# Three small tiles move in the order in which a fused attention and feed-forward kernel allocates its on-chip memory

## Chip, cores and metric

One core of one Trainium2 chip. The metric is the device time of the whole kernel in microseconds (us), the median of several runs. Engines are named as in the profile: PE is TensorE's matmul, PEld its weight load, DVE is VectorE, ACT is ScalarE, POOL is GpSimd, SP is SyncE, whose queue issues most of the DMAs.

## What is computed

The input x has 8 x 1024 tokens of 512 channels, the context 8 x 64 tokens of 384 channels. All weights are given.

```python
def reference(x, ctx, Wq, bq, Wk, bk, Wv, bv, Wo, bo, W1, b1, theta, w_real, w_imag, W2, b2):
    # layer 1: cross attention, 16 heads of 32 channels, 64 keys
    q = layernorm(x) @ Wq + bq;  k = ctx @ Wk + bk;  v = ctx @ Wv + bv
    attn = softmax(clip(q @ k.T * 32 ** -0.5, -1e4, 1e4))      # NaN anywhere: 1 / 64
    x = x + (attn @ v) @ Wo + bo
    # layer 2: feed-forward, 2048 hidden channels
    h = layernorm(x) @ W1 + b1
    g = cos(theta) * w_real + sin(theta) * w_imag
    act = relu(h + g * w_imag * sin(theta + 0.1 * h) * 0.1)
    return x + act @ W2 + b2
```

## The kernel before

All 8192 tokens are worked off in 16 tiles of 512 tokens, first all of them through the attention (phase A, 64 groups of 4 heads of a tile), then all of them through the feed-forward (phase B, 16 tiles by 16 chunks of 128 hidden channels). The order of the work on each engine is written out by hand, with a semaphore for each kind of hand-over.

Every large product is made of three matmuls. Each operand is split into a high part in the fp32r format and a low part that holds what is left, and `product` (lines 1040 to 1045) issues high by high, high by low and low by high into one bank of PSUM. The second operand of a matmul call is the moving one, which streams through the array; the first is the stationary one, which is loaded ahead of it.

- The normalised tile is transposed on PE (`transposes`, line 1049), copied out of PSUM by ACT as `xt_hi` (line 611), and DVE makes `xt_lo` of the rest (line 806).
- `queries` (line 1053) has `xt_hi` and `xt_lo` as moving operands against `wq_hi` and `wq_lo`: 12 matmuls of 128 x 512 for each of the 64 groups.
- Scores have `kbd` moving against `q` (128 x 256), the weighted values `pt` against `vbd`, the output projection `wo` against `o`.
- The first product of the feed-forward has `xt` moving again, against `w1a` or `w1b`: 12 matmuls for each of the 256 chunks. `second` (line 1234) has `w2` moving against `act`: 12 more.
- ACT reads the first product twice: `turns` with the bias `u_shift` (line 755) and `hid` with the bias `par` (line 757); DVE, POOL, ACT and DVE again make the sine and the activation of it.
- `minus_half` is the exponent tile of the reciprocal root on POOL (line 463). `par` holds the four vectors of 2048 channels, loaded at the start (line 603); `red` is scratch for them, `u_shift` and `gain` come of them (lines 942 to 955 and 998 to 1006).

Each tile on chip is a range of bytes that is the same in all 128 partitions. Tiles are laid one behind another in the order in which the program names them (lines 128 to 217), each at the next multiple of 32 bytes. The memory of phase A (`pa`) and that of phase B (`pb`) lie at the same place, 91168 and up. Start bytes as they come of the sizes, with the remainders that the text speaks of:

| tile | start | mod 64 | mod 512 |
|---|---|---|---|
| ident | 16512 | 0 | 128 |
| x_sb (2 tiles) | 23232, 31424 | 0 | 192 |
| par, u_shift, minus_half | 39616, 39872, 39936 | 0 | 192, 448, 0 |
| xt_hi, xt_lo | 39968, 48160 | 32 | 32 |
| bq_sb | 56672 | 32 | 352 |
| w1a, wq, kbd, act, w1b, w2, xn | from 58400 and from 91168 | 32 | 32 |
| wk_sb, wv_sb, ctxt | from 58400 | 32 | 32 |
| q, vbd, prob | behind kbd and two small tiles | 32 | 224 |
| pt, o, wo, res | behind three more small tiles | 32 | 96 |

Of the kernel before, what the change touches and what calls it, by code (L numbers as in the profile page):

```python
# [15 lines left out]
P = 128  # L16
# [12 lines left out]
NB = TOK // P  # L29
# [7 lines left out]
FC = FF // P  # L37
# [72 lines left out]
def xattn_ffn(nc, x, ctx_768, wq, bq, wk, bk, wv, bv, wo, bo, w1, b1, phases, w_real, w_imag, w2, b2,  # L110
# [5 lines left out]
    stack = ExitStack()  # L116
    with stack:
# [6 lines left out]
        def sbuf(where, name, shape, dt=F32):  # L124
            return where.enter_context(nc.sbuf_tensor(name, shape, dt))
# [5 lines left out]
        bo_row = sbuf(stack, "bo_row", [P, C])  # L131
        shift_rows = sbuf(stack, "shift_rows", [P, 2, NB])
        x_sb = [sbuf(stack, f"x_sb{i}", [P, NB, C]) for i in range(XBUFS)]
        par = sbuf(stack, "par", [P, 4, FC])
        u_shift = sbuf(stack, "u_shift", [P, FC])
        minus_half = sbuf(stack, "minus_half", [P, NB])
        xt_hi = sbuf(stack, "xt_hi", [P, KC, TOK], F32R)
        xt_lo = sbuf(stack, "xt_lo", [P, KC, TOK], F32R)
        stats = sbuf(stack, "stats", [P, 2, NB, 6])
        mv = sbuf(stack, "mv", [P, 2, NB, 2])  # L140
        var_eps = sbuf(stack, "var_eps", [P, 2, NB])
        rstd = sbuf(stack, "rstd", [P, 2, NB])
        bq_sb = sbuf(stack, "bq_sb", [P, KC])
        bk_sb = sbuf(stack, "bk_sb", [P, KC])
        red = sbuf(stack, "red", [P, 8, FC])
        gain = sbuf(stack, "gain", [P, FC])
        squares = sbuf(stack, "squares", [P, 2 * GROUPS])
        not_nan = sbuf(stack, "not_nan", [P, 2 * GROUPS])
# [1163 lines left out]
```

## Time and profile before

| | |
|---|---|
| median of 3 runs | 2117.81 us (2117.48 to 2121.49) |
| the profiled execution, its own time | 2117.81 us |
| its span, first to last instruction | 2116.1 us |
| outside the span | 1.7 us |
| TensorE, busy share of the span | 99% (2084.9 us) |
| mean granted clock of TensorE | 0.996 |

A matmul's record in this trace is longer than the time from its start to the start of the next, since matmuls are pipelined. So what a matmul costs is read from the distance of two starts in the timeline, not from its duration; the busy time of a group counts overlapping records of that group once, and sums over groups exceed the span.

### The profile page before, as it was taken

To read this page: it belongs to the slowest core of one execution; us is meant where nothing else is said; L and a number is where in the kernel's file an instruction comes from. 1 tells how busy PE (TensorE), PEld (TensorE's weight loads), DVE (VectorE), ACT (ScalarE), POOL (GpSimd) and SP (SyncE) were. 2 spreads that over 40 slices of the span, in tenths; PEclk is the share of its full clock that TensorE was granted. 3 is DMA by queue.
4 is the path that set the end of the run, shared out by engine and by line. 5 is a ranking of instruction groups with operands and counts; after the bars stand their busy time and mean duration, and the time that the engine had idled before them with its cause. 6 is when DMAs were issued, how large, how long until landed. Compare 5 with 4: busy or idle time off the path is not lost.

```text
span 2116.1 us, 27349 instructions
## 1 busy us (share of the span) xinstructions
PE 2084.9 (99%) x9986; PEld 1740.0 (82%) x9986; DVE 1313.4 (62%) x1994; ACT 1142.2 (54%) x2036; POOL 1040.0 (49%) x757
## 2 busy tenths in 40 slices
PE   7999999999999999999999999999999999999999
PEld 5888888888887878888888888888888888888887
DVE  5888888888875755555555555555545555555554
ACT  4766666766664655454454544445454444445543
POOL 4776777777775434353333533435334353443421
PEclk9999999999999999999999999999999999999999
DMA  5132232232213300101001010110101101011000
GB/s 180 56 105 80 86 105 95 76 105 75 75 56 120 100 31 20 40 1 41 14 27 40 1 40 1 40 41 1 41 1 41 40 1 40 1 40 40 1 20 21
DMA packets 54263, 102.49 MB, mean 48 GB/s; under 512 B 4840, under 2 KB 5352, under 8 KB 54128
## 3 DMA queue, kind: packets, MB, share of 16 engines
q1 hardware_dynamic: 52976, 100.17, 14.1%
q8 instruction: 79, 1.29, 0.3%
q10 hardware_dynamic: 1152, 0.56, 0.1%
q14 instruction: 56, 0.46, 0.1%
HBM read 66.10 MB, written 34.62 MB: 48 GB/s over the span
## 4 chain that ended last, share of the span: by engine, by line
PE 90%; ACT 3%; DVE 3%; issue 2%; DMA 1%; POOL 0%; SPq 0%; POOLq 0%; ACTq 0%; DVEq 0%
PE psum L1043 29%; PE psum L1045 28%; PE psum L1044 28%; PE psum L1124 2%; PE psum L1049 2%; DVE hid L989 1%; ACT turns L755 1%; ACT hid L757 1%; DMA ctx_sb<-in_ctx 0%; ACT act_hi L746 0%; DVE prob L896 0%; DVE top L902 0%; ACT frac L742 0%; ACT x_sb L623 0%; DVE total L882 0%
## 5 line engine op out<-in xcount | busy, mean ns | idle before, releaser
L584 POOL TENSOR_TENSOR frac<-turns,frac 128x512 f32<-128x512 f32 x256 | 332.2, 1298 | 859.6 <-DVE frac L1017 859.6
L989 DVE SCALAR_TENSOR_TENSOR hid<-frac,gain,hid 128x512 f32<-128x512 f32 x256 | 321.3, 1255 | 147.8 <-ACT frac L742 146.7
L1043 PE MATMUL psum<-w_hi,act_hi 128*128 128x512 f32 x1024 | 400.8, 391 | 0.0
L1044 PE MATMUL psum<-w_lo,act_hi 128*128 128x512 f32 x1024 | 399.4, 390 | 0.0
L1045 PE MATMUL psum<-w_hi,act_lo 128*128 128x512 f32 x1024 | 399.2, 390 | 0.0
L755 ACT ACTIVATE turns<-psum,u_shift 128x512 f32<-128x512 f32 x256 | 176.4, 689 | 372.0 <-PE psum L1045 330.3
L746 ACT ACTIVATE act_hi<-hid 128x512 fp32r<-128x512 f32 x256 | 161.8, 632 | 348.1 <-DVE hid L989 348.1
L1017 DVE TENSOR_SCALAR frac<-turns 128x512 f32<-128x512 f32 x256 | 109.8, 429 | 323.8 <-ACT turns L755 323.8
L992 DVE SCALAR_TENSOR_TENSOR act_lo<-hid,act_hi 128x512 fp32r<-128x512 f32 x256 | 196.4, 767 | 178.8 <-ACT act_hi L746 178.8
L1045 PEld LDWEIGHTS psum<-w_hi,act_lo 128*128 128x128 f32 x1024 | 192.9, 188 | 40.4
L1043 PEld LDWEIGHTS psum<-w_hi,act_hi 128*128 128x128 f32 x1024 | 192.9, 188 | 39.8
L1044 PEld LDWEIGHTS psum<-w_lo,act_hi 128*128 128x128 f32 x1024 | 192.9, 188 | 39.3
L1043 PE MATMUL psum<-xt_hi,w1a_hi 128*128 128x512 f32 x512 | 199.8, 390 | 0.0
L1044 PE MATMUL psum<-xt_lo,w1a_hi 128*128 128x512 f32 x512 | 199.6, 390 | 0.0
L1045 PE MATMUL psum<-xt_hi,w1a_lo 128*128 128x512 f32 x512 | 199.6, 390 | 0.0
L1045 PE MATMUL psum<-xt_hi,w1b_lo 128*128 128x512 f32 x512 | 199.3, 389 | 0.0
L1043 PE MATMUL psum<-xt_hi,w1b_hi 128*128 128x512 f32 x512 | 199.2, 389 | 0.0
L1044 PE MATMUL psum<-xt_lo,w1b_hi 128*128 128x512 f32 x512 | 199.2, 389 | 0.0
L528 POOL TENSOR_TENSOR prob<-prob,inv 128x1024 f32<-128x1024 f32 x64 | 122.0, 1906 | 112.9 <-DVE inv L884 112.9
L757 ACT ACTIVATE hid<-psum,par 128x512 f32<-128x512 f32 x256 | 174.5, 682 | 0.0
L742 ACT ACTIVATE frac<-frac 128x512 f32<-128x512 f32 x256 | 162.2, 633 | 0.0
L681 ACT ACTIVATE psum<-psum 128x512 f32<-128x512 f32 x128 | 74.5, 582 | 124.1 <-DVE prob L896 124.1
(143 smaller groups left out, 4190.9 us busy)
## 6 DMA issues: line engine op xcount, KB each, us to landing
res<-in_x SPq DMA_DIRECT2D x64, 256.0 KB, 2.8
x_dram<-res SPq DMA_DIRECT2D x64, 256.0 KB, 2.0
x_sb<-x_dram SPq DMA_DIRECT2D x16, 1024.0 KB, 5.5
x_sb<-in_x SPq DMA_DIRECT2D x15, 1024.0 KB, 5.7
out<-x_sb SPq DMA_DIRECT2D x15, 1024.0 KB, 4.2
stage<-in_w SPq DMA_DIRECT2D x32, 256.0 KB, 2.8
v_in<-v_dram SPq DMA_DIRECT2D x16, 128.0 KB, 3.0
x_sb<-in_x SPq DMA_DIRECT2D x4, 256.0 KB, 4.6
```

The costliest lines, as they stand in the source:

```text
L528: pool.tensor_tensor(rows, rows, inv[:, (i - 1) % 2, :].unsqueeze(2) .to_broadcast([P, NB * HG, KEYS]), ALU.mult).then_inc(prob_done, 1)
L584: pool.tensor_tensor(frac[:, j % 2, :], turns[:, j % 2, :], frac[:, j % 2, :], ALU.subtract)\
L742: act.activation(frac[:, j % 2, :], frac[:, j % 2, :], ACT.Sin, scale=SIN_SCALE).then_inc(sin_done, 1)
L746: act.activation(act_hi[:, j % ACTS, :], hid[:, j % 2, :], ACT.Relu).then_inc(act_hi_done, 1)
L755: act.activation(turns[:, j % 2, :], hidden, ACT.Identity, bias=u_shift[:, f:f + 1], scale=0.1 / TWO_PI).then_inc(turns_done, 1)
L757: act.activation(hid[:, j % 2, :], hidden, ACT.Identity, bias=par[:, 3, f:f + 1])\
L989: dve.scalar_tensor_tensor(out=hid[:, j % 2, :], in0=frac[:, j % 2, :], scalar=gain[:, f:f + 1], in1=hid[:, j % 2, :], op0=ALU.mult, op1=A ...
L992: dve.scalar_tensor_tensor(out=act_lo[:, j % ACTS, :], in0=hid[:, j % 2, :], scalar=0.0, in1=act_hi[:, j % ACTS, :].bitcast(F32), op0=ALU. ...
L1017: dve.tensor_scalar(frac[:, j % 2, :], turns[:, j % 2, :], ROUND, ROUND, ALU.add, ALU.subtract)\
L1043: pe.matmul(o, a_hi, b_hi, start=first, stop=False)
L1044: pe.matmul(o, a_hi, b_lo, start=False, stop=False)
L1045: return pe.matmul(o, a_lo, b_hi, start=False, stop=last)
```

## The change

Only the order of declarations changes. `par` and `u_shift`, which stood ahead of `xt_hi`, now stand around `red`, and `minus_half` stands behind `rstd`. No instruction, semaphore, shape or loop is changed.

```diff
         x_sb = [sbuf(stack, f"x_sb{i}", [P, NB, C]) for i in range(XBUFS)]
-        par = sbuf(stack, "par", [P, 4, FC])
-        u_shift = sbuf(stack, "u_shift", [P, FC])
-        minus_half = sbuf(stack, "minus_half", [P, NB])
         xt_hi = sbuf(stack, "xt_hi", [P, KC, TOK], F32R)
         xt_lo = sbuf(stack, "xt_lo", [P, KC, TOK], F32R)
         stats = sbuf(stack, "stats", [P, 2, NB, 6])
         mv = sbuf(stack, "mv", [P, 2, NB, 2])
         var_eps = sbuf(stack, "var_eps", [P, 2, NB])
         rstd = sbuf(stack, "rstd", [P, 2, NB])
+        minus_half = sbuf(stack, "minus_half", [P, NB])
         bq_sb = sbuf(stack, "bq_sb", [P, KC])
         bk_sb = sbuf(stack, "bk_sb", [P, KC])
+        par = sbuf(stack, "par", [P, 4, FC])
         red = sbuf(stack, "red", [P, 8, FC])
+        u_shift = sbuf(stack, "u_shift", [P, FC])
         gain = sbuf(stack, "gain", [P, FC])
```

What it does to the start bytes, by the same rule:

| tile | start before | start after | mod 64 after | mod 512 after |
|---|---|---|---|---|
| xt_hi | 39968 | 39616 | 0 | 192 |
| xt_lo | 48160 | 47808 | 0 | 192 |
| stats, mv, var_eps, rstd | 56352 to 56671 | 56000 to 56319 | 0, 0, 0, 32 | |
| minus_half | 39936 | 56320 | 0 | |
| bq_sb, bk_sb | 56672, 56704 | 56352, 56384 | 32, 0 | |
| par | 39616 | 56416 | 32 | |
| red | 56736 | 56672 | 32 | |
| u_shift | 39872 | 57184 | 32 | |
| gain and all that follow, and all that stand ahead of par | as before | as before | | |

## Rows read from the trace of the kernel before

**Rows 1.** The page: busy time by engine, then granted clock in 40 slices.

```profile
PE 2084.9 (99%) x9986; PEld 1740.0 (82%) x9986; DVE 1313.4 (62%) x1994; ACT 1142.2 (54%) x2036; POOL 1040.0 (49%) x757
...
PEclk9999999999999999999999999999999999999999
```

**Rows 2.** The page: shares of the chain that ended last, by engine.

```profile
PE 90%; ACT 3%; DVE 3%; issue 2%; DMA 1%; POOL 0%; SPq 0%; POOLq 0%; ACTq 0%; DVEq 0%
```

**Rows 3.** Stretches of phase A (first) and B: length, busy time, clock, DMA.

```profile
100.00:500.00 400.00, 397.53 (x2209) 342.72 (x2208) 343.60 (x574) 269.62 (x537) 295.71 (x212) 1.00 0.27 89
...
1500.00:2000.00 500.00, 499.77 (x2242) 414.12 (x2241) 264.50 (x374) 244.72 (x405) 200.96 (x141) 1.00 0.08 26
```

**Rows 4.** Groups: line, engine, operation, tiles, shape, count; busy us, mean ns; idle before.

```profile
L1043 PE MATMUL psum<-xt_hi,w1a_hi 128*128 128x512 f32 x512 | 199.8, 390 | 0.0
...
L1043 PE MATMUL psum<-xt_hi,w1b_hi 128*128 128x512 f32 x512 | 199.2, 389 | 0.0
...
L1043 PE MATMUL psum<-xt_hi,wq_hi 128*128 128x512 f32 x256 | 106.2, 415 | 0.6 <-DVE xt_lo L806 0.6
```

**Rows 5.** Timeline of PE in phase B: start, duration, then the instruction.

```profile
1199.84 0.39 PE L1043 MATMUL psum<-w_hi,act_hi 128*128 128x512 f32 x1
...
1202.56 0.39 PE L1043 MATMUL psum<-xt_hi,w1b_hi 128*128 128x512 f32 x1
...
1205.28 0.39 PE L1043 MATMUL psum<-w_hi,act_hi 128*128 128x512 f32 x1
```

**Rows 6.** Timeline of PE in phase A: values, scores, transposes, queries, output.

```profile
299.34 0.40 PE L1043 MATMUL psum<-pt_hi,vbd_hi 128*128 128x512 f32 x1
...
300.73 0.28 PE L1043 MATMUL psum<-kbd_hi,q_hi 128*128 128x256 f32 x1
...
302.15 1.03 PE L1124 MATMUL psum<-ident,prob 128*128 128x128 f32 x8
...
303.26 0.40 PE L1044 MATMUL psum<-xt_lo,wq_hi 128*128 128x512 f32 x1
...
305.80 0.39 PE L1043 MATMUL psum<-wo_hi,o_hi 128*128 128x512 f32 x1
```

**Rows 7.** Six plain fp32 matmuls: their timeline row, merged, and their group.

```profile
24.16 2.74 PE L1065 MATMUL psum<-wv_sb,ctxt 128*128 128x512 f32 x6
...
L1065 PE MATMUL psum<-wv_sb,ctxt 128*128 128x512 f32 x24 | 10.9, 592 | 0.0
```

**Rows 8.** Groups of PE: transposes out of tiles that start differently.

```profile
L1124 PE MATMUL psum<-ident,prob 128*128 128x128 f32 x512 | 66.5, 273 | 0.0
...
L1049 PE MATMUL psum<-ident,x_sb 128*128 128x128 f32 x256 | 30.8, 273 | 2.4 <-DVE pt_lo L908 2.4
```

**Rows 9.** Groups of ACT and DVE whose operands start at differing remainders.

```profile
L755 ACT ACTIVATE turns<-psum,u_shift 128x512 f32<-128x512 f32 x256 | 176.4, 689 | 372.0 <-PE psum L1045 330.3 <-DVE act_lo L992 41.3
L757 ACT ACTIVATE hid<-psum,par 128x512 f32<-128x512 f32 x256 | 174.5, 682 | 0.0
...
L806 DVE TENSOR_TENSOR xt_lo<-psum,xt_hi 128x512 fp32r<-128x512 f32 x128 | 79.5, 684 | 26.7 <-ACT xt_hi L611 26.7
...
L623 ACT ACTIVATE xn<-x_sb,shift_rows,rstd 128x512 f32<-128x512 f32 x64 | 48.2, 802 | 7.9 <-issue 7.9
...
L623 ACT ACTIVATE x_sb<-x_sb,shift_rows,rstd 128x512 f32<-128x512 f32 x62 | 45.3, 804 | 5.2 <-DVE shift_rows L800 5.2
L633 ACT ACTIVATE q_full<-psum,bq_sb 128x512 f32<-128x512 f32 x64 | 44.2, 691 | 4.1 <-PE psum L1045 4.1
...
L967 DVE TENSOR_TENSOR res<-psum,res 128x512 f32<-128x512 f32 x64 | 43.9, 685 | 21.1 <-PE psum L1045 19.5 <-DMA res<-in_x 1.4
...
L982 DVE TENSOR_TENSOR x_sb<-psum,x_sb 128x512 f32<-128x512 f32 x64 | 39.9, 683 | 2.4 <-PE psum L1045 2.4
```

**Rows 10.** Groups that use the small tiles which move.

```profile
L463 POOL TENSOR_TENSOR rstd<-var_eps,minus_half 128x4 f32<-128x4 f32 x32 | 43.0, 1344 | 7.9 <-DVE var_eps L795 7.9
...
L819 DVE TENSOR_SCALAR red<-par 128x16 f32<-128x16 f32 x1 | 1.2, 1207 | 0.0
```

## The prediction

> **What bounds the kernel now.** I read the page first. TensorE is busy 2084.9 of 2116.1 us, 99%, with its clock granted in every slice [rows 1], and the chain of work that ended last lies on PE for 90% [rows 2]. The next engine, DVE, is busy 62%. So the time is the number of matmuls times the distance from one to the next; a change that leaves PE's pace and its few waits alone leaves the time alone. The windows say the same of each phase: PE is busy 397.5 of 400 us in the middle of phase A and 499.8 of 500 us late in phase B, at full clock [rows 3].
>
> What the reader has to fetch next is PE's pace, from the timeline, by starts. In phase B, twelve matmuls of the second product start in 1202.56 - 1199.84 = 2.72 us, and the twelve of the next first product in 1205.28 - 1202.56 = 2.72 us [rows 5]: 226.7 ns each for 512 columns, whether `w2` or `xt` is the moving operand. At the granted 2.4 GHz, 512 columns take 213.3 ns, so 13.3 ns of each (32 cycles) are something else. In phase A the eleven matmuls of a group's queries behind the first take (305.80 - 303.26) / 11 = 230.9 ns, and the six of the values (300.73 - 299.34) / 6 = 231.7 ns [rows 6].
>
> **The change, part by part.** Nothing is added, removed or reordered on any engine, and no DMA goes past another. Only start bytes differ. The parts are what reads or writes a tile that moved.
>
> *The moving operand `xt`.* It is the only thing on the bounding engine that moves. The matmuls that stream it are 3 x 512 + 3 x 512 in phase B and 3 x 256 in phase A [rows 4], together 3840, and at 226.7 ns they are 870 us, 41% of the span. Its start goes from 32 to 0 modulo 64 and from 32 to 192 modulo 512. Every nanosecond per matmul is therefore 3.84 us, or 0.18%; nothing hides it. No row shows an fp32r moving operand that starts at a multiple of 64 bytes, so this price is bounded from both sides.
> - Below: the plain fp32 matmuls of the context. Six of them, merged, last 2.74 us, so the starts are (2.74 - 0.59) / 5 = 0.430 us apart [rows 7]. My estimate is that such a matmul is two streams of 512 columns: 215 ns each, 1.7 over the array's time. If the 13.3 ns of the fp32r matmuls came of the start byte, the most that could be given back is 226.7 - 215 = 11.7 ns, times 3840 = 45 us.
> - Above: the values products, where `pt` starts at 96 and `vbd` at 224 modulo 512, so that the two streams are out of step; they run at 231.7 ns, 5.0 more than `xt` against `w1a`, where both start at 32. Times 3072 in phase B, 15 us; the queries already run at 230.9.
>
> I take 0, for four reasons. First, the plain matmuls of [rows 7] read operands that start at 32 modulo 64 as well, and pay almost nothing; a line crossed every 64 bytes would cost them too. Second, the scores: twelve matmuls of 256 columns start in 302.15 - 300.73 = 1.42 us [rows 6], 118.3 ns each, 11.7 over the array's 106.7. Half the columns carry 11.7 of the 13.3 ns, so nearly all of the surplus is paid per matmul and not per line of memory: what grows with the columns is at most 2 x 1.6 = 3.2 ns, times 3840 = 12 us. Third, transposes out of `prob` (32 modulo 64) and out of `x_sb` (0 modulo 64), both against `ident` at 0, have the same mean, 273 ns [rows 8]; there the second operand is in step with `ident` once and out of step once. Fourth, the output projection, with both operands at 96 modulo 512, and the queries, with both at 32, sit in the same 231 ns pattern, so the remainder itself does not show. The weak point is the values' 231.7: it stands in the same range as its neighbours, which are in step, so I read it as phase A's mix of short and long matmuls and not as a price of the offset, but with six matmuls in a row it is no proof.
>
> The Trainium skill states, in "TensorE: Matmul & The Clock Gate", section "Wait — 56ns, not 53.3ns?", that warm back-to-back matmuls start N / 2.4 GHz plus about 2.5 ns apart, 215.7 ns for 512 columns. The trace's plain fp32 agrees with that; its fp32r, at 226.7, does not. By the skill's figure on all 3840 the sum would be 42 us less; this is named again with the rival below.
>
> *The writers of `xt`.* ACT writes `xt_hi` and DVE `xt_lo`, 128 times each, the latter at 684 ns. DVE's adding out of PSUM takes 685 ns into `res` (32 modulo 64) and 683 ns into `x_sb` (0 modulo 64), ACT's normalising 802 ns into `xn` (32) and 804 ns into `x_sb` (0) [rows 9]. So the start byte is worth at most 2 ns, 128 x 2 = 0.3 us, behind a PE that never waits in phase B. Taken as 0.
>
> *The biases.* `u_shift` and `par` go from 0 to 32 modulo 64. ACT with a bias at 32 (`bq_sb`) takes 691 ns, with `u_shift` at 0 it takes 689 and with `par` at 0 it takes 682 [rows 9]. Even 9 ns on each of 512 would be 4.6 us, on an engine that stands idle 330 us waiting for PE just before `turns`, 1.3 us for each chunk. Taken as 0. If that cover were gone, all 4.6 us would show.
>
> *The small rest.* The root with `minus_half`, 32 x 1.34 us on POOL, starts on the same remainder as before (0 modulo 64); of these only the two whose wait shows are near the path. The chain over `par`, `red` and `gain` runs once; it has some 20 instructions of sixteen columns, its first takes 1.2 us [rows 10], and 20 such would be 24 us, so that 10% off on every one is at most 2.4 us. The four loads of `par` are the same DMAs into another place, and nothing asks for them before step 13 of the 64 of phase A. Taken as 0.
>
> The sum: 2117.81 (the profiled execution, 2116.1 of span and 1.7 around it, which is also the median of the three) + 0 = 2117.8 us. PE's pace is regular to the nanosecond, so I expect no drift from other orders of arrival.
>
> **The rivals.**
>
> *Faster: xt's new start takes away the surplus.* Mechanism: fp32r is streamed in aligned lines of 64 bytes, and an operand that starts in the middle of one needs one more fetch. For it: 32 extra cycles are just one for each of the 32 lines of a 512-column row, and all fp32r operands of this kernel start at 32 modulo 64. Against it: the scores, and the plain matmuls. In full it gives 2117.8 - 45 = 2073 us; if only the part that grows with the columns goes, 2117.8 - 12 = 2106. It decides from 4.2 / 3840 = 1.1 ns per matmul. By the skill's 2.5 ns the full case would be 2076. Chance 0.12 for a gain of over 0.2%, of which 0.07 is for a time below 2110.
>
> *Slower: the two streams of PE lose their step.* Mechanism: PE reads the moving operand of one matmul and the stationary one of the next out of the same memory at the same time. Before, both start at the same remainder modulo 512 in both products of phase B; after, `xt` is at 192 and `w1a`, `w1b` and `wq` at 32, and the reads meet on the same part of it. For it: the values products, the only 512-column ones out of step, are the slowest in phase A by a little, and the pace of phase B is steadier than anything in A. Against it: `prob` and `x_sb` alike against `ident`, and 227 ns within a product while the stationary tile steps on by 512 bytes each time. Price: 3072 x 5.0 = 15 us, 2133 us; it decides from 1.4 ns per matmul of phase B. At twice that price it would be 2148 us. Chance 0.28 for over 0.2% slower, of which 0.10 is for a time above 2135.
>
> *The change moves something but an engine off the path takes it.* ACT or DVE on the moved tiles get slower or faster by tens of ns. PE does not see it: same time, within the 0.60 for no change.
>
> **How the numbers follow.** No measurable change 0.60, slower 0.28, faster 0.12. Measurable means over 0.2%, 4.2 us, which is also how far the three runs before lie apart. The time is that of the likeliest case, 2117.8. The range is to leave out the 0.07 below and the 0.10 above: 2110 to 2135; it holds the out-of-step case at its own price of 2133, and of the faster rival only its small forms. The likeliest case alone has 2114 to 2122.
>
> **What would show it.** In the changed kernel's timeline of phase B, the twelve matmuls of a first product span 2.72 us, as do those of a second: that is the whole claim. If the first product's span is shorter while the second's stays, the faster rival holds (2.58 in full); if it is longer (2.78), the slower one. PE's count stays 9986, and `turns`, `hid` and `xt_lo` keep 689, 682 and 684 ns. The prediction is wrong if PE's distance between starts depends on where an operand begins, which no row here can exclude for fp32r, or if the runs themselves wander by more than the three shown.

## The result, and the profile after

The kernel with the three declarations moved takes 2143.62 us (median of 4 runs, 2139.04 to 2145.38) against 2118.34 us before (4 runs, 2117.48 to 2121.49). The ratio is 1.0113 with a 95% interval of 1.0095 to 1.0133: slower by 1.1%. The ratios here and below are taken between the two sets of runs and are not the quotient of the two medians beside them, from which they differ by up to 0.1%. The profiled execution took 2143.63 us, its span 2141.9 us, 25.8 more than before. The instructions are the same on every engine, in number and in order.

The page answers to [rows 1] and [rows 2] with the same picture, only longer: the same 9986 matmuls, PE busy for 28 us more, the other engines as before, the clock granted throughout, and the chain more than ever on PE.

```profile
span 2141.9 us, 27349 instructions
...
PE 2112.9 (99%) x9986; PEld 1743.9 (81%) x9986; DVE 1314.4 (61%) x1994; ACT 1142.3 (53%) x2036; POOL 1042.9 (49%) x757
...
PEclk9999999999999999999999999999999999999999
...
PE 93%; DVE 2%; ACT 2%; issue 2%; DMA 0%; POOL 0%; SPq 0%; POOLq 0%; ACTq 0%; DVEq 0%
```

The windows of [rows 3] say where. In the stretch of phase A PE starts 2208 matmuls, one fewer than before; late in phase B, in 500 us, 2204 where there were 2242, 1.7% fewer, and it is busy for the same 499.77 us. PE does not wait more. It runs slower while busy, at the same clock.

```profile
100.00:500.00 400.00, 397.59 (x2208) 342.79 (x2207) 342.97 (x574) 268.50 (x533) 294.83 (x213) 1.00 0.27 89
1500.00:2000.00 500.00, 499.77 (x2204) 407.19 (x2203) 256.97 (x360) 238.51 (x395) 193.47 (x136) 1.00 0.08 26
```

The timeline of PE in phase B, against [rows 5], shows which matmuls. The twelve of a first product now take 1203.93 - 1201.12 = 2.81 us where they took 2.72, 234 ns each for 226.7. The twelve of the second product take 1206.66 - 1203.93 = 2.73 us; the surplus of 0.01 lies in the first three, which take 1204.62 - 1203.93 = 0.69 us (230 ns each), and the rest is back at 227.

```profile
1201.12 0.40 PE L1043 MATMUL psum<-xt_hi,w1b_hi 128*128 128x512 f32 x1
...
1203.93 0.39 PE L1043 MATMUL psum<-w_hi,act_hi 128*128 128x512 f32 x1
...
1204.62 0.39 PE L1043 MATMUL psum<-w_hi,act_hi 128*128 128x512 f32 x1
...
1206.66 0.40 PE L1043 MATMUL psum<-xt_hi,w1b_hi 128*128 128x512 f32 x1
```

I summed the distances from each PE start to the next over the whole timeline (one profiled execution of each kernel), by the product that the earlier one belongs to. From before to after, in us: first products 697.7 to 718.4 (+20.7), second products 700.0 to 702.8 (+2.8), queries 183.5 to 186.2 (+2.7), output projection 186.7 to 185.0 (-1.7), the 72 matmuls of the context 24.9 to 27.2 (+2.3), values, scores and transposes together -0.2, PE's first start 0.7 earlier. That is the 25.8 of the span. The context's share is not the change's: these matmuls run once, right at the start, and the runs below that give the whole loss back have it too. What the moved tiles cost is about 24 us, most of it, 20.7 us, in the first product.

The groups that the prediction set at 0 are at 0: `turns` and `hid` with their biases moved, and `xt_lo` with its target moved, have the mean durations of [rows 9] within 2 ns, and the idle time ahead of `turns` has grown, since ACT waits for a slower PE.

```profile
L755 ACT ACTIVATE turns<-psum,u_shift 128x512 f32<-128x512 f32 x256 | 175.9, 687 | 395.6 <-PE psum L1045 354.9 <-DVE act_lo L992 40.4
L757 ACT ACTIVATE hid<-psum,par 128x512 f32<-128x512 f32 x256 | 174.5, 681 | 0.0
...
L806 DVE TENSOR_TENSOR xt_lo<-psum,xt_hi 128x512 fp32r<-128x512 f32 x128 | 79.7, 683 | 28.8 <-ACT xt_hi L611 28.5
```

### The profile page after: what moved, and what is told of

Same layout as the page of the kernel before. It is cut to its first block, busy times and chain, and to the rows that moved or that the text cites. A ratio compares the mean times of both kernels' runs of the same rounds, so it can differ in the third digit from the quotient of the medians.

```text
span 2141.9 us, 27349 instructions
## 1 busy us (share of the span) xinstructions
PE 2112.9 (99%) x9986; PEld 1743.9 (81%) x9986; DVE 1314.4 (61%) x1994; ACT 1142.3 (53%) x2036; POOL 1042.9 (49%) x757
## 4 chain that ended last, share of the span: by engine, by line
PE 93%; DVE 2%; ACT 2%; issue 2%; DMA 0%; POOL 0%; SPq 0%; POOLq 0%; ACTq 0%; DVEq 0%
PE psum L1044 29%; PE psum L1043 29%; PE psum L1045 29%; PE psum L1124 2%; PE psum L1049 2%; ACT turns L755 1%; ACT hid L757 0%; DMA ctx_sb<-in_ctx 0%; DVE prob L896 0%; DVE top L902 0%; PE psum L1080 0%; ACT x_sb L623 0%; DVE total L882 0%; DVE pt_lo L908 0%; PE psum L1164 0%
## 5 line engine op out<-in xcount | busy, mean ns | idle before, releaser
L1043 PE MATMUL psum<-w_hi,act_hi 128*128 128x512 f32 x1024 | 401.4, 392 | 0.0
L1045 PE MATMUL psum<-w_hi,act_lo 128*128 128x512 f32 x1024 | 400.2, 391 | 0.0
L1043 PEld LDWEIGHTS psum<-w_hi,act_hi 128*128 128x128 f32 x1024 | 192.8, 188 | 42.5
L1045 PEld LDWEIGHTS psum<-w_hi,act_lo 128*128 128x128 f32 x1024 | 192.5, 188 | 41.3
L1045 PE MATMUL psum<-xt_hi,w1b_lo 128*128 128x512 f32 x512 | 203.5, 398 | 0.0
L1045 PE MATMUL psum<-xt_hi,w1a_lo 128*128 128x512 f32 x512 | 203.3, 397 | 0.0
L1043 PE MATMUL psum<-xt_hi,w1a_hi 128*128 128x512 f32 x512 | 202.3, 395 | 0.3 <-DVE xt_lo L806 0.3
L1043 PE MATMUL psum<-xt_hi,w1b_hi 128*128 128x512 f32 x512 | 201.9, 394 | 0.0
```

Source lines behind the costliest of these rows:

```text
L1043: pe.matmul(o, a_hi, b_hi, start=first, stop=False)
L1045: return pe.matmul(o, a_lo, b_hi, start=False, stop=last)
```

## The experiments

The words used below: the **step** of a matmul is the start byte of its moving operand less that of its stationary operand. The change takes the step of `xt` against all its weights from 0 to 160 modulo 256 and 512. Unused tiles, "pads", shift the rest. In kernels with pads the three lines of `product` are numbered 2 higher (1 higher in the third), L1045 to L1047 for L1043 to L1045.

### The small tiles alone

```diff
 # the kernel after
+        pad_front = sbuf(stack, "pad_front", [P, 88])        # 352 bytes
         xt_hi = sbuf(stack, "xt_hi", [P, KC, TOK], F32R)
...
         ok_count = sbuf(stack, "ok_count", [1, 1], I32)
+        pad_tail = sbuf(stack, "pad_tail", [P, 40])          # 160 bytes
```

> The small tiles (par, u_shift, minus_half, and with them stats, red and the biases) stand where the change puts them, in the same order, but an unused tile keeps xt_hi at 39968, its start before, and a second unused tile keeps the large weights at the same remainder modulo 512 (all 512 bytes further on). Theory 'xt': only the start of xt counts, so the twelve matmuls of a first product take 2.72 us as before and the time is that of the kernel before, ratio 1.000 within 0.002. Theory 'small tiles': the placement of par, u_shift or red costs, so the ratio stays near 1.011 and a first product stays at 2.81 us.

Measured: 2118.98 us against 2117.38, ratio 1.0011 (1.0002 to 1.0021). The first product takes 1203.12 - 1200.40 = 2.72 us.

```profile
1200.40 0.39 PE L1045 MATMUL psum<-xt_hi,w1b_hi 128*128 128x512 f32 x1
...
1203.12 0.39 PE L1045 MATMUL psum<-w_hi,act_hi 128*128 128x512 f32 x1
```

So it is the start of `xt`. The 0.1% left is at the edge of what is measured, and the run on the period below, with the small tiles moved too, doesn't repeat it.

### The start by itself, or the step

Two kernels, on which the two theories of the prediction's rivals contradict each other. One gives `xt` back its remainder modulo 64 but leaves it out of step; the other takes all tiles to 0 modulo 64 and leaves them in step.

```diff
 # the kernel after
+        pad_front = sbuf(stack, "pad_front", [P, 8])         # 32 bytes
         xt_hi = sbuf(stack, "xt_hi", [P, KC, TOK], F32R)
...
         ok_count = sbuf(stack, "ok_count", [1, 1], I32)
+        pad_tail = sbuf(stack, "pad_tail", [P, 120])         # 480 bytes
```

> The kernel after the change, with 32 unused bytes ahead of xt_hi: it starts at 39648, 32 modulo 64 and 224 modulo 512, while the weights stay at 32 modulo 512 (512 bytes further on). Theory 'line': what costs is a moving fp32r operand that starts at 0 modulo 64, so the pace is back at 226.7 ns and the ratio to the kernel before is 1.000. Theory 'step': what costs is that xt and the weights start at different remainders modulo 512, so the first product stays at 2.81 us and the ratio near 1.011.

Measured: 2142.33 us against 2117.38, ratio 1.0127 (1.0110 to 1.0144). As slow as the change, with `xt` at 32 modulo 64.

```diff
 # the kernel before
         minus_half = sbuf(stack, "minus_half", [P, NB])
+        pad_front = sbuf(stack, "pad_front", [P, 8])         # 32 bytes
         xt_hi = sbuf(stack, "xt_hi", [P, KC, TOK], F32R)
```

> The kernel before the change, with 32 unused bytes ahead of xt_hi, so that xt and every tile behind it (w1a, wq, act, w1b, w2, kbd, pt, wo and all others) start 32 bytes further on: all at 0 modulo 64, all still in step with each other modulo 512. Theory 'line': now both products of phase B and all of phase A have a moving operand at 0 modulo 64, so both take 2.81 us for twelve matmuls and the ratio is near 1.02 (twice the change's loss, with 6144 matmuls of phase B at 7 ns more, 43 us). Theory 'step': still in step, ratio 1.000.

Measured: 2118.2 us against 2117.38, ratio 1.0005 (0.9995 to 1.0014). As fast as before, with everything at 0 modulo 64. The timeline of the first kernel (the padded `xt`) and then of this one:

```profile
1201.11 0.40 PE L1045 MATMUL psum<-xt_hi,w1b_hi 128*128 128x512 f32 x1
...
1203.91 0.39 PE L1045 MATMUL psum<-w_hi,act_hi 128*128 128x512 f32 x1
```

```profile
1203.69 0.39 PE L1044 MATMUL psum<-xt_hi,w1b_hi 128*128 128x512 f32 x1
...
1206.41 0.39 PE L1044 MATMUL psum<-w_hi,act_hi 128*128 128x512 f32 x1
```

2.80 us with the step at 192, 2.72 us with the step at 0. The 'line' theory fell in both, the 'step' theory held in both.

### PE alone, over all steps

A kernel that computes nothing of the reference and streams 48 matmuls for each pair of starts, with no other engine at work:

```python
# 6: moving starts at 160, stationary at 0, modulo 512; 512 columns, fp32r
for n in range(48):
    m = pe.matmul(psum[:, 6, 0:512], sta[:, 0, 0 + 128 * (n % 4):128 + 128 * (n % 4)],
                  mov[:, n % 4, 40:552], start=n == 0, stop=n == 47)
```

> No work of the reference is done; the output is the first tile of x, 16 times. One engine alone: 56 groups of 48 back-to-back fp32r matmuls, each group with one start of the moving operand and one of the stationary operand modulo 512, mostly 512 columns. Theory 'line': pace 226.7 ns when the moving operand starts at 32 modulo 64 and 233 to 234 ns when at 0 modulo 64, whatever the stationary one does. Theory 'step': 226.7 ns when both starts are the same modulo 512 and about 234 ns otherwise, so of the first 16 groups (stationary at 0) only the first is fast, of the next 16 (stationary at 32) only the second. A third way: all groups run at one pace, and the change's loss needs the other engines' accesses to memory.

Each group is one merged row, and a group's pace is the distance to the next group's start over 48. The rows below are, in order: stationary at 0 with the moving operand at 0, 32, 64, 96, 128, 160, 192, 224, 256; then stationary at 32 with the moving operand at 0, 32, 64.

```profile
27.58 11.04 PE L57 MATMUL psum<-mov,sta 128*128 128x512 f32 x48
38.46 11.37 PE L60 MATMUL psum<-mov,sta 128*128 128x512 f32 x48
49.66 11.16 PE L63 MATMUL psum<-mov,sta 128*128 128x512 f32 x48
60.66 11.37 PE L66 MATMUL psum<-mov,sta 128*128 128x512 f32 x48
71.87 11.36 PE L69 MATMUL psum<-mov,sta 128*128 128x512 f32 x48
83.07 11.40 PE L72 MATMUL psum<-mov,sta 128*128 128x512 f32 x48
94.31 11.35 PE L75 MATMUL psum<-mov,sta 128*128 128x512 f32 x48
105.50 11.35 PE L78 MATMUL psum<-mov,sta 128*128 128x512 f32 x48
116.69 11.05 PE L81 MATMUL psum<-mov,sta 128*128 128x512 f32 x48
127.58 11.37 PE L84 MATMUL psum<-mov,sta 128*128 128x512 f32 x48
...
205.81 11.35 PE L105 MATMUL psum<-mov,sta 128*128 128x512 f32 x48
217.00 11.05 PE L108 MATMUL psum<-mov,sta 128*128 128x512 f32 x48
227.88 11.37 PE L111 MATMUL psum<-mov,sta 128*128 128x512 f32 x48
239.09 11.16 PE L114 MATMUL psum<-mov,sta 128*128 128x512 f32 x48
```

| step, bytes | pace, ns (stationary at 0) |
|---|---|
| 0 | (38.46 - 27.58) / 48 = 226.7 |
| 32 | 233.3 |
| 64 | 229.2 |
| 96 | 233.5 |
| 128 | 233.3 |
| 160, that of the change | (94.31 - 83.07) / 48 = 234.2 |
| 192 | 233.1 |
| 224 | 233.1 |
| 256 | 226.9 |

What the reader is to see: the fast group moves with the stationary operand (start 217.00, both at 32), so among starts at multiples of 32 bytes it is the difference that counts and neither start by itself; and it comes again at 256, so the period is 256 bytes, not the 512 of my theory, in which the second 16 groups too had only one fast one. The step of the change gives 234.2 ns here, without ACT, DVE, POOL or DMA, and 234 in the full kernel: the loss is PE's own. It is two reads of PE, since the pace depends on where the stationary tile starts as well: with the moving operand at 0 and the stationary one 8 bytes further on it was 230.8 ns. Each group ran once, but the eight steps of the table come again at 256 to 480 bytes, and with the stationary tile at 32, within 0.2 ns; with the moving operand at 0 and the stationary one at 64, 128 or 256, the difference holds within 1 ns. The pair of the change itself, moving at 192 and stationary at 32, ran at 234.2.

The Trainium skill says in "TensorE: Matmul & The Clock Gate", section "Step-by-step: what each phase is for", that PE has two independent read ports, one for the streamed operand and one for the weights. These groups do not agree for fp32r: the pace depends on the two starts together, by up to 7.5 ns in the table, which two reads that have nothing to do with each other would not give; the measurement decides. That two reads meet in one part of the memory is my explanation and is not shown; the runs show the dependence alone.

### Finer steps, and other types

> No work of the reference is done; the output is the first tile of x, 16 times. Stationary operand at 0 modulo 256, moving operand at every multiple of 4 bytes from 0 to 252 (fp32r, 512 columns, 64 groups of 36), then every 32 bytes with 256 columns, plain fp32 with 512 columns, and bf16 with 512 columns. Theory 'step of 256': the pace depends on the difference alone, with a lowest value of 226.7 ns at 0 and at a few places near 0 (28 was one) and 229 to 240 ns elsewhere; nothing is below 226.7. Since plain fp32 is slower per byte read, its pace stays within 1 ns of 429 ns at all starts. For bf16, half the bytes per column: I expect no dependence, 215 to 217 ns. Rival 'line': the pace follows the moving start modulo 16 or 64 alone, so the 64 groups repeat with that period.

Measured with groups of 36, the stationary operand at 0: 226.7 to 226.9 ns at steps 0, 28, 60, 156, 236, 240 and at 252 (227.2); elsewhere 228 to 239; the worst, 240 ns, at 20, 132, 196 and 244. No repetition after 16 or 64 bytes, and nothing below 226.7. The first seven rows are steps 0 to 24 in fours, the next ones plain fp32 at 0 and 32 and bf16 at 32 and 64.

```profile
30.09 8.32 PE L64 MATMUL psum<-mov,sta 128*128 128x512 f32 x36
38.26 8.68 PE L67 MATMUL psum<-mov,sta 128*128 128x512 f32 x36
46.77 8.55 PE L70 MATMUL psum<-mov,sta 128*128 128x512 f32 x36
55.16 8.40 PE L73 MATMUL psum<-mov,sta 128*128 128x512 f32 x36
63.40 8.50 PE L76 MATMUL psum<-mov,sta 128*128 128x512 f32 x36
71.74 8.80 PE L79 MATMUL psum<-mov,sta 128*128 128x512 f32 x36
80.38 8.57 PE L82 MATMUL psum<-mov,sta 128*128 128x512 f32 x36
...
612.10 20.76 PE L280 MATMUL psum<-mov,sta 128*128 128x512 f32 x48
632.69 20.76 PE L283 MATMUL psum<-mov,sta 128*128 128x512 f32 x48
...
722.86 7.93 PE L298 MATMUL psum<-mov,sta 128*128 128x512 bf16 x35
730.63 7.93 PE L301 MATMUL psum<-mov,sta 128*128 128x512 bf16 x35
```

Plain fp32 takes (632.69 - 612.10) / 48 = 429 ns at each of five steps, bf16 (730.63 - 722.86) / 36 = 215.8 ns at each of the six whose next start can be read. Neither depends on the step, at the steps tried, which were all multiples of 32 bytes. With 256 columns fp32r goes between 117.7 (step 64 or 192) and 119.8 ns (step 0 or 96): there step 0 is not the best.

The theory's "difference alone" holds for starts at multiples of 32 bytes and fails on finer ones. Both pairs below have a difference of 240 modulo 256. In the first sweep, with the moving operand at 0 and the stationary one at 16, the pace is (507.15 - 495.95) / 48 = 233.3 ns:

```profile
495.95 11.36 PE L183 MATMUL psum<-mov,sta 128*128 128x512 f32 x48
507.15 11.36 PE L186 MATMUL psum<-mov,sta 128*128 128x512 f32 x48
```

In this one, with the moving operand at 240 and the stationary one at 0, it is (541.46 - 533.30) / 36 = 226.7 ns:

```profile
533.30 8.32 PE L244 MATMUL psum<-mov,sta 128*128 128x512 f32 x36
541.46 8.80 PE L247 MATMUL psum<-mov,sta 128*128 128x512 f32 x36
```

All tiles of this kernel start at multiples of 32, so for them the difference is enough.

### The period, in the kernel

```diff
 # the kernel after
+        pad_front = sbuf(stack, "pad_front", [P, 24])        # 96 bytes
         xt_hi = sbuf(stack, "xt_hi", [P, KC, TOK], F32R)
...
         ok_count = sbuf(stack, "ok_count", [1, 1], I32)
+        pad_tail = sbuf(stack, "pad_tail", [P, 104])         # 416 bytes
```

> The kernel after the change with 96 unused bytes ahead of xt_hi: xt starts at 288 modulo 512, the weights at 32, so they are 256 bytes out of step. Theory 'step of 256' (by the sweep, where a difference of 256 runs at 226.7 ns like one of 0): the pace is back at 226.7 ns and the ratio to the kernel before is 1.000 within 0.002, with par, u_shift and minus_half where the change puts them. Rival 'other engines': in the full kernel ACT, DVE and DMA read and write beside PE, and the one-engine sweep does not carry over; then the first product stays above 2.75 us.

Measured: 2118.22 us against 2117.26, ratio 1.0003 (0.9993 to 1.0013), and 1206.70 - 1203.98 = 2.72 us for a first product. The changed order of declarations with 96 unused bytes ahead of `xt_hi` is as fast as the kernel before.

```profile
1203.98 0.39 PE L1045 MATMUL psum<-xt_hi,w1b_hi 128*128 128x512 f32 x1
...
1206.70 0.39 PE L1045 MATMUL psum<-w_hi,act_hi 128*128 128x512 f32 x1
```

### A step that costs little by the sweep

The same with 160 bytes ahead of `xt_hi` and 352 behind `ok_count`: the step is 64.

> The kernel after the change with 160 unused bytes ahead of xt_hi: xt starts at 96 modulo 256, the weights at 32, so the step is 64 bytes, for which both sweeps show 228.8 ns. Theory 'step of 256, by the table of the sweep': a first product of 12 matmuls takes 12 x 228.8 = 2.75 us, and the time is 2.1 ns x 3072 = 6.5 us above the kernel before, with one to three us for the slow start of the product that follows it: ratio 1.003 to 1.005, about a third of the change's loss. Rival 'in step or not': any step other than 0 costs the same in the full kernel, ratio 1.011.

Measured: 2137.13 us against 2116.82, ratio 1.0089 (1.0068 to 1.0111). My expectation of about 9 us was less than half of what was measured, and the timeline shows which part I had set too low:

```profile
1202.03 0.40 PE L1045 MATMUL psum<-w_hi,act_hi 128*128 128x512 f32 x1
...
1204.80 0.40 PE L1045 MATMUL psum<-xt_hi,w1b_hi 128*128 128x512 f32 x1
...
1205.74 0.39 PE L1046 MATMUL psum<-xt_lo,w1b_hi 128*128 128x512 f32 x1
...
1207.57 0.40 PE L1045 MATMUL psum<-w_hi,act_hi 128*128 128x512 f32 x1
```

The first product takes 2.77 us: its first four matmuls 0.94 us, 235 each, and the other eight 1.83 us, 229 each, which is the sweep's pace. The second product, whose own step is 0, takes 1204.80 - 1202.03 = 2.77 us, 4 ns more on each than before. So a product in which the step is 64 leaves PE in a state from which the next one needs ten or so matmuls to come back to 226.7. Over the timeline the first products cost 9.6 us more than before (6.5 expected) and the second ones 10.8 (1 to 3 expected). The pace of a long stream of one step is not the price of a short one; changing the step has its own price. It depends on the step that came before: in the mean over phase B, the second product is back at 227 after three matmuls behind a step of 160, after five behind 192 and after ten behind 64. With the change itself (step 160) this part is only 2.8 us. Why it differs is not shown.

### All of phase A in step

By the same reading phase A had two things to give back: the values products, with a step of 128, and the output projection, which is in step but comes after the queries at another remainder. Two kernels, from the one before:

```diff
+        pad_q = sbuf(pa, "pad_q", [P, 16])                   # 64 bytes, in the first of the two
         q_hi = sbuf(pa, "q_hi", [P, 2, TOK], F32R)
         q_lo = sbuf(pa, "q_lo", [P, 2, TOK], F32R)
         q_full = sbuf(pa, "q_full", [P, TOK])
+        pad_v = sbuf(pa, "pad_v", [P, 16])                   # 64 bytes, in the second instead
         v_in = sbuf(pa, "v_in", [P, 2, C])
...
+        pad_pt = sbuf(pa, "pad_pt", [P, 32])                 # 128 bytes, in both
         pt_hi = sbuf(pa, "pt_hi", [P, PAIRS, TOK], F32R)
```

> The kernel before with 64 unused bytes ahead of q_hi and 128 ahead of pt_hi, so that q, vbd, prob, pt, o and wo too start at 32 modulo 256 and every pair of operands of every product is in step. Theory 'step': the values products go from 231.7 to 227 or so (384 x 5 = 1.9 us), the output projection loses the slow start that follows a change of remainder (768 x 3 to 4 = 2.7 us); the scores with 256 columns go from 118.3 to 120.0 by the first sweep (768 x 1.7 = 1.3 us lost); in all 3 us faster, ratio 0.9985, at the edge of what can be measured. Rival 'mix': phase A's 231 ns come of the mix of short and long matmuls, not of starts; then no row changes and the ratio is 1.000.

> As e6_phase_a_in_step, but q stays at 224 modulo 256 against kbd at 32 (the 64 unused bytes stand behind q_full). Theory 'step': the gains of the values and the output projection as there, and the scores stay at 118.3 ns, so about 4.5 us faster, ratio 0.998. Rival 'mix': ratio 1.000.

Measured: the first 2115.36 us against 2117.26, ratio 0.9989 (0.9980 to 0.9998); the second 2111.36 us, ratio 0.9969 (0.9957 to 0.9982). The second is faster than both kernels of this study. Its timeline: output projection, values, scores, transposes.

```profile
400.05 0.39 PE L1045 MATMUL psum<-wo_hi,o_hi 128*128 128x512 f32 x1
...
402.77 0.39 PE L1045 MATMUL psum<-pt_hi,vbd_hi 128*128 128x512 f32 x1
...
404.13 0.28 PE L1045 MATMUL psum<-kbd_hi,q_hi 128*128 128x256 f32 x1
...
405.54 1.03 PE L1126 MATMUL psum<-ident,prob 128*128 128x128 f32 x8
```

The output projection takes 2.72 us and the values 404.13 - 402.77 = 1.36 us, both 226.7 ns; in [rows 6] the values took 1.39. The scores take 1.41 us. With q in step too they take 1.43, from the timeline of the first kernel, and as the sweep of 256 columns says:

```profile
407.41 0.28 PE L1045 MATMUL psum<-kbd_hi,q_hi 128*128 128x256 f32 x1
...
408.84 1.03 PE L1126 MATMUL psum<-ident,prob 128*128 128x128 f32 x8
```

Theory 'mix' fell for the values and the output projection: their 231 ns were a matter of starts.

It did not fall for the queries, which follow the transposes. Their operands are in step in all three kernels, and their first ten or so distances are slow in the kernel before and in the first of these two alike, 224 to 236 ns. Over the timeline they take 183.5 us before, 184.4 in the first and 181.7 in the second; 768 matmuls at 226.7 would be 174. In the second kernel they are back at 227 after three distances. That is worth 2.7 us against the first kernel, and the scores are worth 2.0, of the 6.4 us between the two profiled executions. The two kernels differ only in where `q` starts; why that shortens the settling of a later product is not shown.

## Why the prediction was wrong

What bounds the kernel, and that only the moving operand `xt` can matter, was right: 3840 matmuls, nothing hiding a nanosecond of them. The writers, the biases, the small tiles and the DMAs cost nothing that can be told, as set. What failed is the step "I take 0" for the price of `xt`'s start; it was 6.7 ns for each of 3072 matmuls of phase B (20.7 us over the timeline), with 2.8 us on the second products behind them and 2.7 us on the queries, less 1.7 us that the output projection gained. What costs is not the start by itself but its difference from the start of the weights. The four reasons that I gave for the 0, one by one:

- The plain fp32 matmuls of [rows 7] and the transposes of [rows 8] said nothing: the fine sweep has plain fp32 at 429 ns at every step tried. They were the nearest rows by shape, but of another type, and the dependence is fp32r's alone among the three types. The transposes were also misread: `ident` starts at 128, `x_sb` at 192 and `prob` at 224 modulo 512, so neither pair was in step. No run varied the starts of transposes.
- From the scores I read that the surplus of 13.3 ns at step 0 is paid per matmul. The scores stood at a step of 64, not 0 (`kbd` at 32, `q` at 224), so the comparison mixed two steps; the sweep at step 0 bears the reading out, with 119.8 ns for 256 columns, 13.1 over the array's 106.7. It answers another question. It speaks against a gain, and I let it exclude a loss: 226.7 ns was the lowest value of both sweeps for 512 columns, and the trace of before had nothing else in phase B to tell me so.
- That output projection and queries, in step at different remainders, "sit in the same 231 ns pattern, so the remainder itself does not show" was read the wrong way round. The remainder of a product by itself does not count, but a change of it from one product to the next does: with all remainders equal the output projection runs at 226.7. The queries' 231, at a step of 0, was the settling behind the transposes.
- The values' 231.7 ns, which I called phase A's mix, was a price of the step, as the weak point said it might be. A step of 128 costs 233.3 in a long stream.

The rival on the other side, "the two streams of PE lose their step", named the right place and the right condition, that the two operands no longer start in step; that their reads meet on the same part of the memory is not shown by any run. Its price, 5.0 ns for 3072 matmuls and 2133 us, was too low: six matmuls of the values at a step of 128 stood for a step of 160, whose pace is 234.2. Its period of 512 bytes was wrong, it is 256. Against it I had set that 227 ns holds while the stationary tile steps on by 512 bytes, which is two whole periods and no evidence at all. `prob` and `x_sb` against `ident`, the other point set against it, were both out of step. The faster rival's mechanism, lines of 64 bytes, fell with the second and third experiments, so its 2073 had nothing behind it.

The range ended at 2135, since I put only 0.10 above it; the measured 2143.6 needs 6.7 ns for each of 3840 matmuls. The range's upper end was the mean of six values matmuls; the longest single distance among the six, 0.24 us from the first start to the second, would have covered it.

## What to carry to other kernels

Where PE is busy all the time with fp32r products, the start bytes of the two operands belong to the tuning: for 512 columns let their difference be a multiple of 256, with the same remainder for products that follow each other (for 256 columns a step of 64 was faster here, 1.41 us against 1.43 for twelve); a small tile declared in between undoes it silently. Measure the pace as the distance of starts for each product, since the durations of matmuls and the busy share hide it. And where a stretch runs at a perfectly regular pace, ask whether it is the norm or the best case before pricing an edit at nothing.

## What the runs showed of the hardware

- fp32r matmuls of 512 columns, each with its weight load, start 226.7 ns apart when the moving and the stationary operand start at the same byte modulo 256, and mostly 228 to 240 ns apart otherwise (240 at step 20), with a few other steps of 4 bytes, such as 28 and 60, as fast as 0. Multiples of 32 bytes, which is where tiles start here, give 229.2 at 64 and 233 to 234.2 at all others but 0; among them only the difference counts, while for finer starts the same difference of 240 gave 226.7 and 233.3.
- bf16 at 215.8 ns and plain fp32 at 429 ns show no such dependence at steps that are multiples of 32 bytes.
- After a product of another step, or after transposes, PE needs up to ten matmuls to settle, mostly 224 to 236 ns each: three behind a step of 160, five behind 192, ten behind 64. This is why step 64, at 229 in a long stream, cost 0.9% in the kernel.
- What exactly the two reads of PE share was not settled. The pattern over 4-byte steps has no simple form (226.7 at 240 and 240 at 244), and no run took the weight loads away.
